# The last chunk of the last pass in two halves, two multiplies on GpSimd, and an earlier read of the check's outcome

## The reference, cut to what matters

```
x0 = x
x1 = adj @ x0
x2 = 2 * (adj @ x1) - x0            # the same for the second support, which is adj again
out = concat(x0, x1, x2, x1, x2) @ weight + bias
x = layernorm(x + out)              # over the 64 features, eps 1e-5, no scale or shift
```

## Time and profile before

| | us |
|---|---|
| median of 3 runs | 1260.37 (1260.17 to 1260.38) |
| the profiled execution, its own time | 1260.2 |
| its span in the profile | 1258.2 |
| PE busy in the span | 1228.9 (98%) |
| DVE busy | 758.8 (60%) |
| ACT busy | 215.5 (17%) |
| POOL busy | 62.0 (5%) |
| mean granted clock of PE | 0.996 of full speed |

### The profile page before, as it was taken

The page is one execution under the profiler, slowest core; times in us unless marked ns, Lnnn a source line. Parts: engine busy times, 40 slices in busy tenths (PEclk is TensorE's granted clock), DMA queues, the critical chain, the costliest instruction groups (busy, mean ns, idle before and its releaser), DMA issues.

```text
span 1258.2 us, 16358 instructions
## 1 busy us (share of the span) xinstructions
PE 1228.9 (98%) x5872; PEld 1028.3 (82%) x5872; DVE 758.8 (60%) x1863; ACT 215.5 (17%) x392; POOL 62.0 (5%) x52
## 2 busy tenths in 40 slices
PE   8999999999999999999999999999999999999996
PEld 6888888788878887878888888878888888888875
DVE  5836897787776777778635554462246255544624
ACT  5622111121111101120111111020111111110110
POOL 0000000000000000000000001010000000010100
PEclk9999999999999999999999999999999999999998
DMA  9832112211111110101011032033001111320320
GB/s 342 327 101 60 38 49 65 72 45 39 52 55 55 47 38 24 44 22 43 15 34 34 20 90 64 13 105 80 1 27 42 34 34 28 86 64 9 95 58 36
DMA packets 128646, 78.16 MB, mean 62 GB/s; under 512 B 97312, under 2 KB 108064, under 8 KB 126752
## 3 DMA queue, kind: packets, MB, share of 16 engines
q1 hardware_dynamic: 128560, 77.05, 21.1%
HBM read 53.42 MB, written 23.59 MB: 61 GB/s over the span
## 4 chain that ended last, share of the span: by engine, by line
PE 90%; DVE 6%; DMA 2%; issue 1%; SPq 1%; ACT 1%; DVEq 0%; ACTq 0%
PE ps L672 29%; PE ps L673 29%; PE ps L776 20%; PE ps L690 8%; PE ps L711 2%; PE ps L712 2%; DVE nat L1038 1%; DVE ring L1038 1%; DMA raw<-in_at 1%; PE ps L684 1%; DVE xs L936 1%; DVE sml L980 0%; SPq L1080 0%; ACT xs L810 0%; DVE sml L971 0%
## 5 line engine op out<-in xcount | busy, mean ns | idle before, releaser
L672 PE MATMUL ps<-B,xs 128*128 128x512 f32 x1664 | 654.9, 394 | 4.2 <-DVE xs L936 4.2
L673 PE MATMUL ps<-B,xs 128*128 128x512 f32 x1664 | 648.0, 389 | 0.0
L672 PEld LDWEIGHTS ps<-B,xs 128*128 128x128 f32 x1664 | 312.6, 188 | 67.9 <-ACT xs L810 3.9
L673 PEld LDWEIGHTS ps<-B,xs 128*128 128x128 f32 x1664 | 312.7, 188 | 62.3
L776 PE MATMUL ps<-Tw,xs 128*128 128x512 f32 x1280 | 309.3, 391 | 2.5 <-DVE ring L1038 2.5
L776 PEld LDWEIGHTS ps<-Tw,xs 128*128 128x128 f32 x1280 | 238.6, 188 | 55.1 <-DVE ring L1038 4.6
L924 DVE TENSOR_TENSOR ring<-ps,rrep 128x512 f32<-128x512 f32 x94 | 64.5, 689 | 252.7 <-PE ps L673 244.2
L1038 DVE SCALAR_TENSOR_TENSOR nat<-ps,embn,nat 128x128 f32<-128x128 f32 x448 | 153.6, 343 | 51.1 <-PE ps L776 50.8
L1038 DVE SCALAR_TENSOR_TENSOR ring<-ps,embn,ring 128x128 f32<-128x128 f32 x512 | 175.0, 342 | 0.0
L690 PEld LDWEIGHTS ps<-W,ring 128*128 128x128 f32 x896 | 111.5, 191 | 12.0 <-DVE ring L924 3.7
L690 PE MATMUL ps<-W,ring 128*128 128x128 f32 x896 | 113.2, 275 | 4.4 <-DVE ring L924 2.5
(11 more groups left out here) (66 smaller groups left out, 542.9 us busy)
## 6 DMA issues: line engine op xcount, KB each, us to landing
raw<-in_at SPq DMA_DIRECT2D x13, 1024.0 KB, 16.2
td<-ring SPq DMA_DIRECT2D x32, 256.0 KB, 2.0
ring<-td SPq DMA_DIRECT2D x128, 64.0 KB, 2.5
ring<-in_xn SPq DMA_DIRECT2D x16, 256.0 KB, 2.9
ring_x<-in_xt SPq DMA_DIRECT2D x32, 128.0 KB, 3.2
ring_x<-y1d SPq DMA_DIRECT2D x32, 128.0 KB, 3.2
out<-nat SPq DMA_DIRECT2D x16, 256.0 KB, 2.3
y1d<-ring SPq DMA_DIRECT2D x14, 256.0 KB, 2.8
```

Of the source, the lines that this page charges most:

```text
L672: pe.matmul(bank, x[:, 0, m, :], of, start=m == 0, stop=False)
L673: mm = pe.matmul(bank, x[:, 1, m, :], of, start=False, stop=ends and m == NT - 1)
```

## The change

**1. Two halves.** A table `SPAN` of column ranges is added: chunks 0 to 3 of 512 columns, and chunks 4 and 5, which are the halves (256 columns each) of chunk 3. All helpers (`ch`, `pe_quarter`, `pe_weighed`, `scale`, `centre`, ...) take their width from it. In pass 6 of pair 1 alone, chunk 3 is replaced by 4 and 5, each with a product bank and an `after` bank of its own, and its half of the slots for the scaled chunk and the squares.

**2. A hand-written order for the end of pair 1, pass 6,** with the outs moved up from the end of the list to behind each `normed`.

**3. The final multiply of chunks 1 and 2 on POOL** (`pooled`); DVE takes their reciprocals only.

**4. The flag is read by ACT, DVE, POOL and SP behind the step `scale 1 6 1`** (`CUT`). The rest of the fast way is the Else of `If(v != 0)`; on SP, too, the fast rest now stands in the Else. In the If, DVE first issues the `scale` and `after` steps that PE's fast way waits for. PE still runs its whole fast way and reads the flag at its end.

```diff
+SPAN = [(512 * c, 512) for c in range(NC)] + [(1536, 256), (1792, 256)]
...
-            if p == 6 and j != 1:
+            if p == 6:
                 put("out", j, 6, c)
...
+        if (j, p) == (1, 6):
+            order = order[:12]
...
+        if (j, p) == (1, 6):
+            for m in range(4):
+                put("mm", j, p, 4, m)
+                if m == 1:
+                    put("after", j, p, 2)
+                    put("deviate", j, p, 1)
+                    put("centre", j, p, 2)
+            put("scale", j, p, 4)
+            put("normed", j, p, 1)
+            exchange(1)
+            put("mm", j, p, 5, 0)
+            put("mm", j, p, 5, 1)
+            put("deviate", j, p, 2)
+            put("normed", j, p, 2)
+            exchange(2)
+            put("after", j, p, 4)
+            put("centre", j, p, 4)
+            put("mm", j, p, 5, 2)
+            put("mm", j, p, 5, 3)
+            put("scale", j, p, 5)
+            put("deviate", j, p, 4)
+            put("after", j, p, 5)
+            put("centre", j, p, 5)
+            put("normed", j, p, 4)
+            exchange(4)
+            put("deviate", j, p, 5)
+            put("normed", j, p, 5)
+            exchange(5)
+            return
...
-        if j == 1:
-            for c in range(NC):
-                put("out", j, 6, c)
...
-END = STEPS.index(Step("out", 1, 6))
+CUT = STEPS.index(Step("scale", 1, 6, 1)) + 1
+
+def pooled(s):
+
+    return (s.j, s.p) == (1, 6) and s.c in (1, 2)
...
+            def within(slot, c):
+
+                return slot[:, 256 * (c - 4):256 * (c - 3)] if c > 3 else slot
...
             def pe_quarter(pe, x, bank, c, k, ends):
                 for m in range(4 * k, 4 * k + 4):
-                    of = B[:, m, c * 512:(c + 1) * 512]
+                    of = B[:, m, span(c)]
...
-            def pe_weighed(pe, bank, *pairs):
-                for k in range(4):
+            def pe_weighed(pe, bank, c, *pairs):
+                for k in range(SPAN[c][1] // P):
...
+                        if c == 4:
+                            dv.wait_ge(s_norm, norm_at[Step("normed", j, p, 0)])
+                        if c == 5:
+                            dv.wait_ge(s_pn, pool_at[Step("normed", j, p, 1)])
                         dv.tensor_reduce(sm[:, 0, :], g, axis=AX.X, op=ALU.add).then_inc(s_sum, 1)
...
                         dv.reciprocal(sm[:, 0, :], sm[:, 3, :]).then_inc(s_rec, 1)
-                        dv.wait_ge(s_rec, norm_at[s])
+                        if pooled(s):
+                            continue
+                        dv.wait_ge(s_rec, rec_at[s])
...
+                    if s.kind == "normed" and pooled(s):
+                        po.wait_ge(s_rec, rec_at[s])
+                        po.tensor_tensor(g, g, sml[:, n, c, 0, :].unsqueeze(2).to_broadcast([P, 8, C]),
+                                         ALU.mult).then_inc(s_pn, 1)
...
                     if s.kind == "out":
-                        sp.wait_ge(s_norm, norm_at[Step("normed", j, 6, c)])
+                        normed = Step("normed", j, 6, c)
+                        sp.wait_ge(*((s_pn, pool_at[normed]) if pooled(normed) else (s_norm, norm_at[normed])))
...
             @block.vector
             def _(eng):
-                fast.dve(eng, STEPS)
+                fast.dve(eng, STEPS[:CUT])
                 eng.wait_ge(s_flag, 1)
                 v = eng.value_load(flag[0:1, 0:1], min_val=0, max_val=N)
                 with eng.If(v != 0):
+
+                    fast.dve(eng, [s for s in STEPS[CUT:] if s.kind in ("scale", "after")])
                     eng.memset(bad[:], 0.0).then_inc(s_here, 1)
                     eng.wait_ge(s_here, 4)
                     slow.dve_start(eng)
                     slow.dve(eng, STEPS)
+                with eng.Else():
+                    fast.dve(eng, STEPS[CUT:])
...
             @block.sync
             def _(eng):
-                fast.sp(eng, STEPS[:END])
+                fast.sp(eng, STEPS[:CUT])
                 eng.wait_ge(s_flag, 1)
                 v = eng.value_load(flag[0:1, 0:1], min_val=0, max_val=N)
-                with eng.If(v == 0):
-                    fast.sp(eng, STEPS[END:])
-                with eng.Else():
+                with eng.If(v != 0):
                     fast.sp_start(eng)
                     slow.sp_start(eng)
                     slow.sp(eng, STEPS)
+                with eng.Else():
+                    fast.sp(eng, STEPS[CUT:])
```

More of the change, by code:

```diff
@@ L463, in way @@
             prep2_at = {s: 2 * v for s, v in numbered("prep2").items()}
-            mean_at, var_at, norm_at = numbered("centre"), numbered("deviate"), numbered("normed")
+            mean_at, var_at, rec_at = numbered("centre"), numbered("deviate"), numbered("normed")
+            norm_at = {s: i + 1 for i, s in enumerate(s for s in rec_at if not pooled(s))}
+            pool_at = {s: i + 1 for i, s in enumerate(s for s in rec_at if pooled(s))}
             n_T = len(T_at)
@@ L574, in way @@
                         sq_after[s] = held_q[n]
-                        held_q[n] = (s_var, var_at[Step("deviate", s.j, s.p, s.c)])
+                        if s.c != 4:
+                            held_q[n] = (s_var, var_at[Step("deviate", s.j, s.p, s.c)])
             def tile_landed(m, c):
@@ L584, in piece, with span @@
                 return slice(c * width, (c + 1) * width)
+            def span(c):
+                return slice(SPAN[c][0], sum(SPAN[c]))
+            def within(slot, c):
+                return slot[:, 256 * (c - 4):256 * (c - 3)] if c > 3 else slot
             def ch(t, c):
-                return t[:, c * 512:(c + 1) * 512]
+                return t[:, span(c)]
             def groups(t, c):
@@ L611, in y_slot @@
                             ring[:, 4, :], ring[:, 5, :], ring_x[:, 0, :], ring_x[:, 1, :]][4 * j + c]
-                return ring[:, 4 + j % 2, :]
+                return within(ring[:, 4 + j % 2, :], c)
             def square_slot(j, p, c):
@@ L618, in square_slot @@
                     return rrep[:, 1536:2048] if general else ring_g[:]
-                return ps[:, 6 + j % 2, :]
+                return within(ps[:, 6 + j % 2, :], c)
             def part_slot(c):
@@ L674, in pe_quarter, with pe_rest @@
                 return mm
-            def pe_rest(pe, x, bank, v):
+            def pe_rest(pe, x, bank, c, v):
                 for m in range(NT):
                     pe.wait_ge(s_glo, 16 * (v - 1) + m + 1)
-                    pe.matmul(bank, x[:, 0, m, :], glo[:], start=False, stop=m == NT - 1).then_inc(s_gmm, 1)
+                    pe.matmul(bank, x[:, 0, m, :], glo[:, 0:SPAN[c][1]], start=False, stop=m == NT - 1).then_inc(s_gmm, 1)
             def pe_turned(pe, bank, src):
@@ L950, in dve_steps @@
                         dv.wait_ge(s_four, four_at[s])
-                        bank = ps[:, nbank_of[s, "four"], :]
+                        bank = ps[:, nbank_of[s, "four"], 0:SPAN[c][1]]
                         if p == 3:
@@ L961, in dve_steps @@
                             if p == 6:
-                                dv.wait_ge(s_v, v_at[after(j, 5, c)])
+                                dv.wait_ge(s_v, v_at[after(j, 5, min(c, 3))])
                             else:
@@ L1119, in sp_steps @@
                     j, p, c, k, n = s.j, s.p, s.c, s.k, s.j % 2
-                    cols = slice(c * 512, (c + 1) * 512)
+                    cols = span(c)
                     if s == STEPS[0] and not general:
@@ L1227, in _ @@
             def _(eng):
-                fast.act(eng, STEPS)
+                fast.act(eng, STEPS[:CUT])
                 eng.wait_ge(s_flag, 1)
@@ L1254, in _ @@
                     slow.pool(eng, STEPS)
+                with eng.Else():
+                    fast.pool(eng, STEPS[CUT:])
             @block.sync
             def _(eng):
-                fast.sp(eng, STEPS[:END])
+                fast.sp(eng, STEPS[:CUT])
                 eng.wait_ge(s_flag, 1)
                 v = eng.value_load(flag[0:1, 0:1], min_val=0, max_val=N)
-                with eng.If(v == 0):
-                    fast.sp(eng, STEPS[END:])
-                with eng.Else():
+                with eng.If(v != 0):
                     fast.sp_start(eng)
```

37 lines of the change are left out of this document (21 added, 16 removed).

## The result

| | before | after |
|---|---|---|
| median of 18 runs each, us | 1261.31 (1260.17 to 1263.31) | 1256.77 (1254.64 to 1259.81) |
| ratio, with its 95% interval | 1 | 0.9962 (0.9955 to 0.9969) |
| the profiled execution, its own time | 1260.2 | 1257.36 |
| its span | 1258.2 | 1254.9 |

The kernel became 0.38% faster: 4.8 us of the 1260.37 against which the forecast was made, so 1255.6 where 1255.4 was forecast. The interval is 0.9 us to either side, so an agreement to 0.2 us is finer than these runs can tell. (The kernel before ran 15 more times beside the changed one; that is why its median is now 1261.31.)

The account below looks back on a forecast made before the run. PE, busy 98% of the span, bounds the kernel until its last matmul, then the end does. Terms -2.7 + 0.8 - 2.83 - 0.2 = -4.9 from 1260.2 give 1255.3, with 0.17 for the median 1255.4 us; range 1254.4 to 1257.9.

Parts of the forecast that it names:

- Part 1: Flag read moved from behind the last landing to mid-stream: -2.7 us, with DVE's 3.5 us stall hidden in idle time.
- Part 2: Chunk 3's product on PE as 64 matmuls of 256 columns, 0.120 us each: last product ready 0.8 us later.
- the bound of 0.226: Upper bound for a 256-column matmul on PE: no cheaper than 512 columns, 0.226 us.
- Part 3: Tail from the last product to the last multiply's end: 4.67 us against 7.50, so -2.83.
- Free by a hair: DVE's queue ends at 1245.76, just ahead of the last product at 1245.8; up to 0.3 us of lateness possible.
- Part 4: Two multiplies on POOL, 1.30 us each against 0.69 on DVE: cost 0, and 1.4 us taken off DVE.
- Part 5: Last output, 128 KB instead of 256, lands in 2.4 us instead of 2.6: -0.2.
- The span of 1253.3: Sign that the forecast is right: the profiled execution's span comes out at 1253.3 us.
- A: DVE and POOL block each other near the last scale: 0.2 to 0.3 late, 1255.7; hard form 1256.7. Chance 0.35.
- B: The flag-read stall is longer in mid-stream, up to twice 3.5 us; PE waits about 2.4: 1257.8. Chance 0.08.
- C: The fall out of the Else at the end costs as much as the jump did: 1258.1. Chance 0.06.
- D: 256-column matmuls on PE are no cheaper, 0.226 us each: 6.8 us more, 1262.2, slower. Chance 0.05.

Follow-up runs that it names:

- e1: The changed kernel without the halves and without POOL's multiplies, so the early flag read alone; ratio 0.9980 to the kernel before.
- e7: The kernel before with only SP's If turned round, so the outs stand in the Else; ratio 0.9994 to the kernel before.
- e6: The changed kernel with the flag read one chunk later, behind the scale of chunk 2; ratio 0.9974 to the kernel before.
- e8: The changed kernel with the mean formed and subtracted in one DVE operation; ratio 0.9957 to the kernel before.
- e3: The changed kernel with all multiplies on DVE, none on POOL; ratio 0.9967 to the kernel before.
- e2: The changed kernel with the flag read at the ends as before and SP's If turned back; ratio 0.9984 to the kernel before.
- e10: The changed kernel with the mean fused into the subtract and PE's flag load moved ahead of its last weights matmuls; ratio 0.9964 to the kernel before.
- e4: The changed kernel with chunk 3 whole instead of in halves; ratio 0.9961 to the kernel before.
- e5: The changed kernel with four more POOL multiplies into unused columns; single execution, chunk 1's scale to last multiply's end 23.38 us against the change's 21.87.
- e9: The changed kernel with PE's flag load moved ahead of its last weights matmuls, branch still at the end; ratio 0.9976 to the kernel before.

## Why the prediction was right

**Part 1, the flag read: right, at its size.** -2.7 forecast, 3.14 to 0.49 measured, and e1 with e7 divide it: 1.7 for SP's jump, the rest once DVE's is gone as well, which the prediction had not separated. The stall was taken at 3.5; DVE's branch to its next operation is 1234.52 - 1231.6 = 2.9. The first operation was forecast 4.4 us behind chunk 1's `scale` and came 3.83 behind it. The queue behind it, told as six large operations, is five large and two small ones in the trace; its 3.65 us were right. That it is hidden, and why, was right (e1), and e6 shows the price where the cover is missing.

**Part 2, the halves on PE: right.** 0.120 us a matmul forecast, 0.12 measured; the bound of 0.226 was far off. Four weights records 0.71 for 0.72. The last product is 0.84 later by e8, forecast 0.8.

**Part 3, the tail: right.** -2.86 for -2.83. DVE at 256 columns took 0.42 as read off the line between 128 and 512. "Free by a hair" held: 0.07 us late.

**Part 4, POOL: right in cost, off in a duration.** The multiplies take 1.05 and 1.04 us, not the 1.30 of the earlier trace rows, which are additions: the nearest row was of another operation. The sum had no term for their worth; e3 puts it at 0.99 us.

**Part 5, the last landing: the one term that was mis-sized.** 2.4 forecast, 1.9 measured in the change. The range of 2.2 to 2.9 that I read off held neither 1.9 nor the 3.2 to 3.8 of e2, e3, e6 and e8 to e10. The rows were of 256 KB outs; the last of these met PE's second fetch in none of the kernels (2.3 to 2.6 in before, e1, e4 and e7). The step that failed is "the one of chunk 4 is issued 1.4 us ahead and should be out of the way": I asked only which outs lie beside the last one, and not what else the DMA engines carry. The other half is Part 1's sentence that PE's jump ends before the landing: it does (1253.1 against 1254.5), but the fetch comes behind it. The kernel before held a sign of it. The 2.9 of the earlier trace rows is its out of chunk 2, issued at 1247.6, when PE's first fetch began (1247.62 to 1249.02): fifteen sixteenths of it had landed by 1249.8, the last at 1250.5. Its DMA view from 1247 to 1251 us:

```profile
q8 instruction: 1, 0.02, 2.2%
...
out<-nat SPq DMA_DIRECT2D x1, 256.0 KB, 2.9
```

By the second row of the table above, a drain 0.3 us earlier would have made the time some 1.5 us longer: still in the range, and near its end.

**What was luck.** That the change stands on the good side of this fetch was not foreseen. The stretch fell by 5.3 where 4.9 was forecast, and the median time by 4.8; that the two numbers 1255.6 and 1255.4 lie so close is in part chance. The span of 1253.3 that was named as a sign came out at 1254.9; the 3.4 us at the lower clock, which no term foresaw, are worth 1.7 us of it by the estimate above.

**The rivals.** A is shown (e5), and in the change it has its mild form: 0.07 us at the last `scale` (e8), for the 0.2 to 0.3 given; it was the mean's `tensor_scalar` that was held, just ahead of the subtract. B is refuted: one stall of 2.9, and only 0.68 us were left of the cover. C is refuted: from the landing to the end of the span, with the fall out of the Else and the drain, it is 0.5. D is refuted by 0.12.

## What to carry to other kernels

A jump at the end of a program has a price on each engine, and the one on the path hides the next (e7): move all of them, and put each where its engine waits anyway, checked against the row that is next due on it (e1 against e6). Count the transfers of code as transfers: a fetch among the first packets of the last output cost 1.3 us or more here in the landing. And when work moves to POOL, look at what DVE reads while it runs, small operations too.

## What the runs showed that I had not expected

- A jump to far code takes PE 3.3 to 3.9 us in these profiles, DVE 2.9 to 3.5, SP 2.5 to 2.8, and it moves 16 KB of instructions twice on PE, each in one transfer of 0.9 to 1.6 us.
- A fetch of 16 KB held up one sixteenth of an output until it was done: 1.9 us to landing became 3.2 to 3.8.
- In ten of the fourteen profiles TensorE's clock was at its lower level for 3.4 us once or twice ahead of the end, and the number of such stretches orders the profiles' times up to chunk 1's `scale` almost without overlap.
- A `tensor_scalar` of 128 x 4 numbers was held by a running POOL multiply for as long as 0.71 us, while a sum over 128 x 256 numbers from SBUF was not held at all.
- In e9, PE's branch took 3.91 us, the longest of all. Its first fetch also took longest there (1.57 us, beside one of 8 KB); whether that is the cause is open.
